# One stage of a graph network: the sum with x0 as a second product in the bank, and the activated rows by ScalarE

## The reference, cut to what matters

```
x0 = jax.nn.relu(node_features @ fc1_w + fc1_b)
x = x0
for i in range(N_LAYERS):
    beta = math.log(THETA / (i + 1) + 1.0)
    h = jax.ops.segment_sum(x[src] * norm[:, None], dst, num_segments=N)
    h = (1.0 - ALPHA) * h + ALPHA * x0
    x = jax.nn.relu((1.0 - beta) * h + beta * (h @ conv_w[i]))
return x @ fc2_w + fc2_b
```

## Time and profile before

| | us |
|---|---|
| median of 3 runs (6315.4 to 6319.56) | 6319.4 |
| the profiled execution | 6320.36 |
| its span | 6318.5 |
| stage `light_and_tail` | 1222 |

### The profile page before, as it was taken

How to read it: one execution, slowest core, us unless ns; L and a number is a source line. 1 busy time by engine, 2 the same in 40 slices (tenths; PEclk the granted TensorE clock), 3 DMA queues, 4 the chain that set the end, 5 groups by cost and what they waited for, 6 DMA issues and landing times. The chain is left out here.

```text
span 6318.5 us, 75199 instructions
## 1 busy us (share of the span) xinstructions
PE 3490.4 (55%) x17463; PEld 2423.7 (38%) x17463; DVE 4195.7 (66%) x16010; ACT 2932.1 (46%) x7129; POOL 3713.9 (59%) x3700
## 2 busy tenths in 40 slices
PE   0525774625430000577777766888699984444443
PEld 0423553625420000344444434656466653343222
DVE  7359996519563697799999987777366654454332
ACT  1945775312200122566667656777466662232110
POOL 0655666656656467653544436666576617676777
PEclk9868998766665555798899988999899995656666
DMA  2224664535412366333544435555244437665333
GB/s 66 77 86 148 200 202 128 172 93 145 116 35 45 93 175 168 105 112 95 111 109 101 108 85 188 187 190 178 86 133 136 133 105 239 190 197 159 121 120 102
DMA packets 512369, 827.34 MB, mean 131 GB/s; under 512 B 108999, under 2 KB 193843, under 8 KB 510796
## 3 DMA queue, kind: packets, MB, share of 16 engines
q1 hardware_dynamic: 396011, 629.55, 30.7%
q0 software_dynamic: 115936, 193.21, 13.6%
HBM read 382.25 MB, written 452.03 MB: 132 GB/s over the span
## 5 line engine op out<-in xcount | busy, mean ns | idle before, releaser
L3038 POOL DMA_INDIRECT gcn_ring<-GT,gcn_index x588 | 587.4, 999 | 199.1 <-issue 170.8
L3139 DVE SCALAR_TENSOR_TENSOR gcn_acc<-gcn_acc,cont,gcn_ring 128x128 f32<-128x128 f32 x588 | 204.5, 348 | 563.9 <-DMA gcn_ring<-GT,gcn_index 562.9
L1575 POOL DMA_INDIRECT light_ring<-C,light_s_u x392 | 383.5, 978 | 327.7 <-DVE light_acc L1618 219.9
L485 POOL DMA_INDIRECT J<-packed,sort_place x392 | 421.8, 1076 | 186.2 <-issue 114.3
L3221 PE MATMUL gcn_psA<-ident,gcn_h 128*128 128x128 f32 x588 | 155.7, 416 | 598.2 <-DVE gcn_h L3142 597.7
L3188 ACT ACTIVATE gcn_hT<-gcn_psA 128x512 f32<-128x512 f32 x147 | 87.8, 597 | 696.8 <-PE gcn_psA L3221 696.4
L3221 PEld LDWEIGHTS gcn_psA<-ident,gcn_h 128*128 128x128 f32 x588 | 100.3, 208 | 636.5 <-DVE gcn_h L3142 636.5
L1418 ACT ACTIVATE tail_h<-tail_x,tail_nmr,tail_std 128x128 f32<-128x128 f32 x784 | 320.7, 483 | 8.6 <-DVE tail_nmr L1349 8.6
L2292 POOL DMA_INDIRECT out<-source_x,source_own_u x196 | 193.7, 988 | 211.9 <-DVE source_x L2378 160.6
L1469 PE MATMUL tail_psT<-ident,tail_h 128*128 128x128 f32 x784 | 144.0, 314 | 266.5 <-ACT tail_h L1418 266.5
L476 POOL DMA_INDIRECT got_s<-TAB,src_u x196 | 207.0, 1056 | 140.3 <-issue 59.5
(11 more groups left out here) (635 smaller groups left out, 13216.4 us busy)
## 6 DMA issues: line engine op xcount, KB each, us to landing
T<-front_t SPq DMA_DIRECT2D x196, 272.0 KB, 2.1
C<-light_acc SPq DMA_DIRECT2D x147, 256.0 KB
source_c<-C SPq DMA_DIRECT2D x147, 256.0 KB
GT<-source_r SPq DMA_DIRECT2D x147, 256.0 KB, 2.3
gcn_own<-GT SPq DMA_DIRECT2D x147, 256.0 KB
RC<-gcn_own SPq DMA_DIRECT2D x147, 256.0 KB
RG<-gat_rows SPq DMA_DIRECT2D x98, 264.0 KB
front_x<-in_x SPq DMA_DIRECT2D x98, 256.0 KB
```

The source lines that it names most:

```text
L485: nc.gpsimd.indirect_dma_start(out=table, out_offset=bass.IndirectOffsetOnAxis(ap=index[:, c:c + 1], axis=0), in_=rows[:, c, :], in_offset ...
L1575: nc.gpsimd.indirect_dma_start(out=ring[:, n % RING, j, :], out_offset=None, in_=tables[h], in_offset=bass.IndirectOffsetOnAxis(ap=index[: ...
L3038: nc.gpsimd.indirect_dma_start(out=ring[:, n % RING, j, :], out_offset=None, in_=net.GT[i], in_offset=bass.IndirectOffsetOnAxis(ap=index[: ...
L3139: nc.vector.scalar_tensor_tensor(out=acc[:, n % 2, j, :], in0=before, scalar=net.cont[:, c:c + 1], in1=ring[:, n % RING, j, :], op0=ALU.mu ...
```

## The change

DVE's `g1T` and `g2T` go. In their place ACT makes `x1T` and `x2T`, the ReLU of the bank alone, and PE makes the sum: (x1 + x0) @ W is x1 @ W + x0 @ W, so the products `conv1` and `conv2` become a pair each, `x0T` first and `x1T` or `x2T` second, added up in the same bank (`both`). The buffers are renamed and keep their sizes. `x0T` has to live until `conv2` has read it, so its wait is on `c3_done` now.

```diff
     def vector_step(self, v, n, early, late):
...
-        m = n - 6
-        if inside(m):
-            v.wait_ge(self.c2_done, m + 1)
-            after(v, self.c3_done, m, 2)
-            nc.vector.scalar_tensor_tensor(out=self.rows(self.g2T, 2, m), in0=ps["C2"][:, :], scalar=0.0, in1=self.rows(self.x0T, 3, m),
-                                           op0=ALU.max, op1=ALU.add).then_inc(self.g2_made, 1)
...
-        m = n - 5
-        if inside(m):
-            v.wait_ge(self.c1_done, m + 1)
-            after(v, self.c2_done, m, 2)
-            nc.vector.scalar_tensor_tensor(out=self.rows(self.g1T, 2, m), in0=ps["C1"][:, :], scalar=0.0, in1=self.rows(self.x0T, 3, m),
-                                           op0=ALU.max, op1=ALU.add).then_inc(self.g1_made, 1)
...
     def scalar_step(self, act, n):
...
             act.wait_ge(self.x0_done, m + 1)
-            after(act, self.g2_made, m, 3)
+            after(act, self.c3_done, m, 3)
             nc.scalar.activation(self.rows(self.x0T, 3, m), ps["F"][:, :], ACT.Relu, bias=w["fc1_b"][:, 0:1], scale=1.0 / X0_SCALE).then_inc(self.x0T_made, 1)
+        m = n - 6
+        if inside(m):
+            act.wait_ge(self.c2_done, m + 1)
+            after(act, self.c3_done, m, 2)
+            nc.scalar.activation(self.rows(self.x2T, 2, m), ps["C2"][:, :], ACT.Relu).then_inc(self.x2T_made, 1)
...
+        m = n - 5
+        if inside(m):
+            act.wait_ge(self.c1_done, m + 1)
+            after(act, self.c2_done, m, 2)
+            nc.scalar.activation(self.rows(self.x1T, 2, m), ps["C1"][:, :], ACT.Relu).then_inc(self.x1T_made, 1)
         root(0, n)
...
     def tensor_step(self, pe, n):
...
+        def both(weight, m, rows_, out, done):
+            nc.tensor.matmul(ps[out][:, :], w[weight][:, :], self.rows(self.x0T, 3, m), start=True, stop=False)
+            nc.tensor.matmul(ps[out][:, :], w[weight][:, :], rows_, start=False, stop=True).then_inc(done, 1)
...
-            pe.wait_ge(self.g2_made, m + 1)
+            pe.wait_ge(self.x2T_made, m + 1)
             if m + 5 <= NODE_GROUPS:
                 pe.wait_ge(self.uT_made, min(m + 5, NODE_GROUPS))
-            columns("conv2", self.rows(self.g2T, 2, m), "U", self.c3_done)
+            both("conv2", m, self.rows(self.x2T, 2, m), "U", self.c3_done)
...
-            pe.wait_ge(self.g1_made, m + 1)
-            after(pe, self.g2_made, m, 1)
-            columns("conv1", self.rows(self.g1T, 2, m), "C2", self.c2_done)
+            pe.wait_ge(self.x1T_made, m + 1)
+            after(pe, self.x2T_made, m, 1)
+            both("conv1", m, self.rows(self.x1T, 2, m), "C2", self.c2_done)
```

More of the change, by code:

```diff
@@ L1291, in __init__ @@
         self.yn, self.h3, self.h2T, self.uT, self.h3T = (ring(n_, 2) for n_ in ("yn", "h3", "h2T", "uT", "h3T"))
-        self.x0T, self.g1T, self.g2T, self.x3T = ring("x0T", 3), ring("g1T", 2), ring("g2T", 2), ring("x3T", 2)
+        self.x0T, self.x1T, self.x2T, self.x3T = ring("x0T", 3), ring("x1T", 2), ring("x2T", 2), ring("x3T", 2)
         self.stats, self.mv, self.std, self.nmr = (sb(n_, [P, 3, self.MV, S, k]) for n_, k in (("stats", 6), ("mv", 2), ("std", 1), ("nmr", 1)))
@@ L1302, in __init__ @@
             "xb_made", "gy_made", "x3_made", "h3_made", "h3_turned", "h3T_made", "x0_done", "x0T_made"))
-        self.c1_done, self.g1_made, self.c2_done, self.g2_made, self.c3_done, self.x3T_made, self.o_done, self.o_made = (sem(n_) for n_ in (
-            "c1_done", "g1_made", "c2_done", "g2_made", "c3_done", "x3T_made", "o_done", "o_made"))
+        self.c1_done, self.x1T_made, self.c2_done, self.x2T_made, self.c3_done, self.x3T_made, self.o_done, self.o_made = (sem(n_) for n_ in (
+            "c1_done", "x1T_made", "c2_done", "x2T_made", "c3_done", "x3T_made", "o_done", "o_made"))
     def rows(self, t, k, m):
@@ L1490, in tensor_step @@
             pe.wait_ge(self.x0T_made, m + 1)
-            after(pe, self.g1_made, m, 1)
+            after(pe, self.x1T_made, m, 1)
             columns("conv_lone", self.rows(self.x0T, 3, m), "C1", self.c1_done)
```

## The result

| | median us | lowest to highest | runs |
|---|---|---|---|
| before | 6317.4 | 6311.0 to 6319.6 | 4 |
| after | 6464.2 | 6459.3 to 6479.1 | 4 |

The ratio is 1.0238, with a 95% interval of 1.0219 to 1.0257: slower by 147 us, where +159 was forecast. The profiled executions took 6,320.4 and 6,460.7 us.

The account below looks back on a forecast made before the run. After the change a loop from ACT to PE and back was to bind: 12.10 us plus 1.64 for PE's low clock, 13.7 a step against 12.06. Over 97 steps +159 on 6,319.4 gives 6,478 us, range 6,345 to 6,545.

Parts of the forecast that it names:

- DVE's relief: On DVE, removing `g2T` and `g1T` at 0.60 us each frees 117.6 us in all, worth nothing to the time.
- The loop of 12.10 us: Written-order path from ACT's `x0T` to PE's `fc1` and back, without DVE: 7.94 us on ACT plus 4.16 on PE.
- `x2T` and `x1T` at 0.47 each: On ACT, each new ReLU copy costs 0.47 us, taken from `x3T`; bounds 0.47 and 0.60.
- A product of a pair at 0.87: On PE, each column product costs 0.87 us at the high clock; the second doesn't wait for the first.
- The low stretch: PE at its low clock (1.2 GHz) after its long gap, once in every step: 1.64 us, giving 13.7 a step.
- none (+4 us): No low clock on PE's part of the loop: 12.1 us a step, against 12.06 today.
- five terms (+373): Turn, `Wu1a`, conv1 twice and `fc1` on PE all at the low clock: 3.8 us more, 15.9 a step.
- Rival A: DVE is the bound and its relief arrives: 6,200 to 6,270 us; chance 0.07.
- Rival B: The loop binds but PE keeps its high clock: 12.1 us a step, 6,323, no change; chance 0.09.
- Rival C: PE's low stretch falls on the path in 6 of 10 steps: 13.1 us a step, 6,418; chance 0.20.
- Rival D: More than one low stretch a step, or second product's weights late: 14.5 us a step and more, 6,556 up; chance 0.04.

Follow-up runs that it names:

- filled_gap: The kernel after with two column products for nothing on PE between conv2 and the turn of `h3`: 6,316 us, ratio to before 1.0012.
- hoist_x2: The kernel after with conv1's `x0T` product issued right behind conv2 and `x2T` ahead of `x0T` in ACT's list: 6,228 us, ratio to before 0.9855.
- x2_first: The kernel after with `x2T` ahead of `x0T` in ACT's list: 6,422 us, ratio to before 1.0169.
- hoist: The kernel after with conv1's `x0T` product issued right behind conv2, in PE's idle time: 6,332 us, ratio to before 1.0024.
- act_only: The kernel after with single products for conv1 and conv2, the sum with x0 left out: 6,386 us, ratio to before 1.0112.
- pairs_only: The kernel before with pairs of products on PE; DVE keeps two instructions, maximum with zero alone: 6,383 us, ratio to before 1.0114.

## Why the prediction was right, point by point

- DVE's relief is worth nothing in this order of lists. Shown: with the clock held high (filled_gap) the kernel is still no faster than before, and hoist_x2, with the same two instructions gone from DVE, is. Its size was wrong, 1.20 us a step for 1.02 measured: the forecast took the two instructions out at 0.60 each and left out that `g1T` had covered a wait. As DVE was not on the path, this did not touch the time.
- The loop of 12.10 us. Shown at 12.15 in filled_gap. The 0.05 is `yn`, 1.82 in place of 1.76, as ACT waits for its end before `x1T`.
- `x2T` and `x1T` at 0.47 each. 0.48 and 0.49 in the timeline, 0.48 by x2_first.
- A product of a pair at 0.87, with no wait of the second for the first. 0.86 in the timeline after, 12.15 - 11.29 = 0.86 by hoist.
- The low stretch, one in every step at 1.64 us. Right in number, a little high in size: 13.65 - 12.15 = 1.50. It is what turned "no change" into a loss, and the weakest step of the argument, a choice between none (+4 us) and five terms (+373). The reason given, that a longer idle time brings a low stretch in every step, holds for this kernel (2.83 us) and not as a rule: act_only idles 3.69 us and has steps that lose nothing (11.29 us) and steps that lose 2.6 (13.9). That it was one in each step here was partly luck. The pace of 13.65 against 13.7 and a mean of 13.57 explain the 12 us between +147 and +159.
- Rival A: DVE's share was as read and the gain absent, until the new work was taken off the loop. By the Trainium skill (Perfetto Trace Analysis, Identifying the Most-Contended Engine) the engine with the highest occupancy comes first; hoist_x2 shows the gain that this promises, the kernel after shows that it needs the loop as well. Rival B is what filled_gap made of the kernel, 6,316. Rival C, a low stretch in 6 of 10 steps, is near to what hoist does, on a loop shorter by 0.86: (12.25 - 11.29) / 1.71 = 0.56. Rival D did not come.
- Of what the profile was to show, three things were off. PE's idle time is 2.83, not 3.0 us. The low stretch lies on the turn, `Wu1a` and the first part of conv1, not on the whole pair. ACT idles in three places, 0.6, 1.1 and 2.1 us (before the root, `uT` and `x0T`), not in one of 3: `uT` waits for `Wu1a`, which the forecast had not looked at. It lies beside the path, so it cost nothing.

## What to carry to other kernels

Before work is moved off the busiest engine, walk the loop that its new homes lie on, in written order, and add up start-to-start distances; occupancy doesn't show it. Put added work where its engine idles on that loop: the same instructions were 2.4% slower than before in one order and 1.5% faster in another. Count the idle time in front of TensorE's critical products as a cost of its own, because what follows it may run at half the clock. And look at what an instruction stands between before it is taken out: it may have covered a wait of its neighbours.

## What the runs showed that was not expected

- Useless work made the kernel after faster by some 145 us, by keeping TensorE's granted clock at its higher level.
- Idle times of TensorE of 1.12 and 1.49 us in front of the turn of `h3` brought no low stretch in any step of the middle of the stage. 1.97 us (hoist) brought one in part of the steps, 2.22 us (pairs_only) in about three of four, 2.35 us (x2_first) in five of six, 2.83 us in practically all. But 3.69 us (act_only) left 17 of 84 steps without one. So the length of this idle time alone doesn't tell; what else decides stays open here.
- Most steps of the kernel after repeat to 0.01 us, at 13.65, whether DVE has no, one or two light sums in them. No run here says why this number is so steady.
